# GpSimd's softplus split into three steps and the first norm's chain into two, in a two-layer recurrent and attention kernel with a new order of steps

## The reference, cut to what matters

```
xn = layernorm(x)
s  = mamba_block(xn)            # layer norm, in_proj, 4-tap causal conv, silu, x_proj,
                                # dt = softplus(dt @ dt_proj_w + dt_proj_b), selective scan over time,
                                # gate, out_proj, then layer norm + gelu FFN
g  = fp4_mlp(xn)                # three linear layers whose inputs are quantized to FP4 in blocks of 16
x  = x + s * silu(g)
xn = layernorm(x)
s  = attention(xn)              # over the batch axis (2 positions), 16 heads
g  = three residual blocks      # linear, layer norm, exact gelu, linear
x  = x + s * silu(g)
```

## Time and profile before

| | |
|---|---|
| median of 3 runs | 1763.05 us (1762.28 to 1764.01) |
| the profiled execution's own time | 1760.51 us |
| its span, first to last instruction | 1757.8 us |
| granted TensorE clock, mean | 0.951 |
| DVE busy | 1559.0 us (89%) |
| PE busy | 1537.0 us (87%) |
| ACT busy | 1437.1 us (82%) |
| POOL busy | 1251.3 us (71%) |

### The profile page before, as it was taken

The page is one execution under the profiler, slowest core; times in us unless marked ns, Lnnn a source line. Parts: engine busy times, 40 slices in busy tenths (PEclk is TensorE's granted clock), DMA queues, the critical chain, the costliest instruction groups (busy, mean ns, idle before and its releaser), DMA issues.

```text
span 1757.8 us, 26243 instructions
## 1 busy us (share of the span) xinstructions
PE 1537.0 (87%) x7512; PEld 1153.3 (66%) x7512; DVE 1559.0 (89%) x2887; ACT 1437.1 (82%) x3076; POOL 1251.3 (71%) x1314
## 2 busy tenths in 40 slices
PE   3766888989898998989898998989898998999875
PEld 2354767767676776667676776767676776777653
DVE  4889999999999999999999999999999999999711
ACT  2466888888998988898998988898998988898632
POOL 2557668787787769687787768687777869686422
PEclk8577999999999999999999999999999999999987
DMA  8111111111111111111111111111111111111100
GB/s 206 51 35 51 46 58 48 49 55 55 43 49 56 54 50 55 49 54 54 44 49 55 52 53 55 50 55 49 42 57 52 47 61 55 43 56 48 31 0 12
DMA packets 68452, 91.58 MB, mean 52 GB/s; under 512 B 15742, under 2 KB 34758, under 8 KB 68310
## 3 DMA queue, kind: packets, MB, share of 16 engines
q1 hardware_dynamic: 64566, 89.73, 17.0%
q10 hardware_dynamic: 3744, 0.18, 0.1%
HBM read 85.17 MB, written 4.72 MB: 51 GB/s over the span
## 4 chain that ended last, share of the span: by engine, by line
POOL 27%; PE 25%; DVE 17%; ACT 16%; issue 13%; DMA 1%; POOLq 0%; ACTq 0%; SPq 0%; DVEq 0%
POOL drive L796 10%; PE bank L339 10%; PE bank L455 6%; DVE unit L960 4%; POOL wide L845 3%; DVE hc L967 2%; ACT unit L571 2%; PE y_ps L365 2%; POOL wide L850 2%; POOL wide L847 2%; ACT hx L550 1%; ACT ops L537 1%; DVE xc L992 1%; ACT L537 1%; PE bank L326 1%
## 5 line engine op out<-in xcount | busy, mean ns | idle before, releaser
L796 POOL TENSOR_TENSOR drive<-wx,rows 128x1024 f32<-128x1024 f32 x256 | 603.6, 2358 | 154.8 <-DMA rows<-rows_scratch 78.5
L960 DVE TENSOR_TENSOR_SCAN unit<-unit,drive 128x512 f32<-128x512 f32 x512 | 616.4, 1221 | 36.5 <-POOL drive L803 27.7
L571 ACT ACTIVATE unit<-dt,aneg 128x254 f32<-128x254 f32 x1024 | 441.8, 468 | 8.0
L967 DVE TENSOR_TENSOR hc<-unit,rows 128x512 f32<-128x512 f32 x512 | 340.5, 683 | 5.6
L365 PE MATMUL y_ps<-ident,hc 128*128 128x128 f32 x2048 | 275.3, 280 | 65.8 <-DVE hc L967 65.7
L365 PEld LDWEIGHTS y_ps<-ident,hc 128*128 128x128 f32 x2048 | 239.1, 144 | 120.0 <-DVE hc L967 79.2
L339 PE MATMUL bank<-w_l,ops 128*128 128x256 f32 x768 | 194.0, 397 | 15.0 <-DVE xc L995 8.9
L339 PEld LDWEIGHTS bank<-w_l,ops 128*128 128x128 f32 x768 | 144.8, 195 | 65.5 <-DVE xc L995 20.5
L571 ACT ACT_TABLE_LOAD x109 | 139.8, 1283 | 1.9
L580 ACT ACTIVATE carry<-unit 128x4 f32<-128x4 f32 x512 | 79.1, 169 | 67.5 <-DVE unit L974 62.8
L455 PE MATMUL bank<-ops,w_f 128*128 128x256 f32 x512 | 116.2, 386 | 10.9 <-ACT ops L537 10.9
(11 more groups left out here) (229 smaller groups left out, 3150.0 us busy)
## 6 DMA issues: line engine op xcount, KB each, us to landing
rows<-rows_scratch SPq DMA_DIRECT2D x256, 256.0 KB, 3.4
x_t<-in_L_attn_x_dram SPq DMA_DIRECT2D x16, 256.0 KB, 3.8
xs<-in_L_attn_x_dram SPq DMA_DIRECT2D x16, 256.0 KB, 3.5
out_dram<-xs SPq DMA_DIRECT2D x16, 256.0 KB, 2.2
w_f<-in_L_attn_ffn_w_dram SPq DMA_DIRECT2D x2, 1024.0 KB
ops<-in_L_ffn_qweights_dram SPq DMA_DIRECT2D x1, 1536.0 KB, 15.2
w_in<-in_L_attn_in_proj_w_dram SPq DMA_DIRECT2D x1, 1024.0 KB, 5.2
hq_t<-attn_in_proj_weight_dram SPq DMA_DIRECT2D x1, 768.0 KB
```

Source lines behind the costliest of these rows:

```text
L571: last = a_.activation(u[:, k * TOK:(k + 1) * TOK].rearrange("p (b t) -> p b t", b=B)[:, :, 1:TC], dt[p][:, g, :].rearrange("p (b t) -> p ...
L796: g_.tensor_tensor(drive[n % 2][:, :, :].rearrange("p (g b) t -> p g b t", b=B), wx[p][:, :, :].rearrange("p g (b t) -> p g b t", b=B), ro ...
L960: v.tensor_tensor_scan(u[:, :], u[:, :], d, 0.0, ALU.mult, ALU.add).then_inc(S["scan_done"], 1)
L967: v.tensor_tensor(hc[n % NPROD][:, 4 * half:4 * half + 4, :].rearrange("p (g b) t -> p g b t", b=B), unit_of(ch, n, half)[:, :].rearrange( ...
```

## The change

Three things change. The three instructions of `log` become steps `log0`, `log1` and `log2`; the chain `f` becomes `fa` (five instructions) and `fb` (five), with the same waits. No instruction is added to POOL or removed. Then all five tables are new. They also begin at another place of the period, so that the signs of many words differ without a change of order.

```
-    "POOL": ("f", "log"),
+    "POOL": ("fa", "fb", "log0", "log1", "log2"),
...
-            elif name == "f":
+            elif name == "fa":
                 pool.wait_ge(*at("f_stats", ch))
                 pool.wait_ge(*at("xhf_done", ch - 1))
...
                 g_.tensor_tensor(r[0], r[3], epsc[:, :], ALU.add).then_inc(S["f_small"], 1)
+            elif name == "fb":
+                mean, var = f_mv[:, :, 0], f_mv[:, :, 1]
+                r = [f_sm[:, k, :] for k in range(8)]
                 pool.wait_ge(*at("f_small", ch, 5))
...
-            elif name == "log":
+            elif name == "log0":
                 pool.wait_ge(*at("sp_act", ch, 1))
                 g_.tensor_scalar(tmp_u, wx[p][:, :, :], 1.0, -1.0, ALU.add, ALU.add).then_inc(S["sp_pool"], 1)
+            elif name == "log1":
                 pool.wait_ge(*at("sp_pool", ch, 1))
                 g_.tensor_tensor(tmp_u, wx[p][:, :, :], tmp_u, ALU.subtract).then_inc(S["sp_pool"], 1)
+            elif name == "log2":
                 pool.wait_ge(*at("sp_pool", ch, 2))
                 pool.wait_ge(*at("dt_act", ch))
                 g_.tensor_tensor(tmp_u, tmp_u, dt[p][:, :, :], ALU.add).then_inc(S["sp_pool"], 1)
```

Two lines of the tables, of DVE:

```
-    clr10b hc11b clr11a attn- clr11b h1- scan12a hc12a scan12b hc12b clr12a clr12b scan13a hc13a clr13a f++
+    clr11b- attn-- scan12a- hc12a- h1-- scan12b- clr12a- hc12b- scan13a- clr12b- hc13a- f+ clr13a- scan13b-
```

More of the change, by code:

```diff
@@ L75 @@
 PE_PLAN = """
[L76 to L79, removed]
+    xn1T-- xi2 xi3 sum7- z1 b0a-- kv-- xp sum8- dt0 q-- b0T-- hqT0- dt1 sum9- b0b-- v1-- hqT1- sum10- sum11-
+    hqT2- h1T-- ctxT-- sum12- b1a-- b2b--- sum13- dn- sum14- b1T-- sum15- ao-- xqT ygT0- skip ygT1- g00 sum0 g01
@@ L80 @@
+    op- sum1 u00 u01 b1b-- g10 sum2 g11 u2T- u10 u11 sum3 h2T-- f10- f11- sum4 f12- f13- b2a-- uT+ sum5 f2-
+    b2T-- sum6 xi0+ xi1+ z0+
 """
 ACT_PLAN = """
[L82 to L85, removed]
@@ L86 @@
-    f13- exp6b out5b u+ exp7a b2n-- out6a exp7b out6b exp8a out7a exp8b b2g-- tap0+ tap1+ hn- z0+ xn1- tap2+
-    tap3+ z1+ out7b out8a xc0+ xc1+ exp9a exp9b out8b exp10a b0n- kv- xp+ out9a out9b exp10b exp11a dt0+ out10a
-    exp11b hq0 b0g- aexp- dt1+ out10b v1- dtexp+
+    b0g-- aexp-- hq0- dt1 v1-- dtexp out10b- exp12a- out11a- out11b- hq1- exp12b- exp13a- out12a- exp13b- hq2-
+    h1-- ctx-- out12b- exp14a- out13a- dtln exp14b- out13b- exp15a- first out14a- out14b- exp15b- b1n-- exp0a
+    gatec--- out15a- gatem- b1g-- exp0b out15b- s1-- xq exp1a out0a out0b yg0- exp1b exp2a yg1- out1a exp2b g00
@@ L89 @@
+    g01 out1b exp3a out2a exp3b out2b exp4a opn- g10 u2- out3a g11 exp4b out3b xn+ exp5a out4a exp5b h2-- out4b
+    exp6a f10- f11- out5a f12- xhf+ f13- exp6b u+ out5b exp7a out6a exp7b b2n-- out6b exp8a out7a exp8b b2g--
+    tap0+ tap1+ hn- z0+ out7b xn1- tap2+ tap3+ xc0+ out8a exp9a exp9b out8b xc1+ z1+ exp10a kv- xp+ b0n- usave+
+    out9a exp10b out9b exp11a out10a exp11b dt0+
 """
 POOL_PLAN = """
-    drive14- drive15- b1-- arg fix0 drive0 xout fin--- drive1 drive2 hb1-- drive3 fix1 f+ drive4 op- drive5 j0in
@@ L92 @@
-    hb2-- drive6 s0b- drive7 b2-- drive8 j0out j1in x1- drive9 drive10 diff- j1out b0- hb0- drive11 xin+ drive12
-    drive13 log+
+    arg drive15- fix0 b1-- drive0 xout fin--- drive1 drive2 fa+ hb1-- drive3 op- drive4 fb+ drive5 j0in hb2--
+    fix1 s0b- drive6 j0out drive7 j1in b2-- drive8 x1- drive9 drive10 diff- j1out hb0- b0- drive11 xin+ drive12
+    drive13 log0+ log1+ drive14 log2+
 """
 DVE_PLAN = """
-    clr15a- xround yg- scan0a clr15b- hc0a scan0b clr0a hc0b clr0b scan1a hc1a clr1a scan1b scan2a hc1b clr1b
@@ L102 @@
[L102 removed]
+    clr11b- attn-- scan12a- hc12a- h1-- scan12b- clr12a- hc12b- scan13a- clr12b- hc13a- f+ clr13a- scan13b-
+    scan14a- hc13b- dt clr13b- hc14a- scan14b- clr14a- hc14b- b1s-- wx clr14b- scan15a- scan15b- hc15a- hc15b-
+    clr15a- xround yg- scan0a clr15b- hc0a scan0b hc0b clr0a clr0b scan1a hc1a scan1b clr1a scan2a hc1b hc2a
+    scan2b clr1b op- hc2b ug0 clr2a scan3a clr2b scan3b h2-- hc3a scan4a hc3b clr3a hc4a clr3b scale0 ug1 scan4b
@@ L1258, in _ @@
                 unscale(1)
-                pool_step(pool, "log", 0)
+                for name in ("log0", "log1", "log2"):
+                    pool_step(pool, name, 0)
                 unscale(2)
```

23 lines of the change are left out of this document (13 added, 10 removed).

## The result

| | before | after |
|---|---|---|
| median | 1762.99 us (1762.28 to 1764.01, 4 runs) | 1776.44 us (1775.11 to 1779.43, 4 runs) |
| the profiled execution's own time | 1760.51 us | 1775.27 us |
| its span | 1757.8 us | 1773.5 us |
| mean granted clock | 0.951 | 0.955 |

The ratio after to before is 1.0078, interval 1.0061 to 1.0096: slower by 13 us or 0.8%, where 1776.0 us was forecast.

What follows compares the result with a forecast made beforehand. No engine is full: a loop through several binds, with DVE near its bound. Its links made a period 1.1 us longer; 1760.51 + 15.4 - 2.5 = 1773.4 us, 1776 us as median, range 1744 to 1797 us.

Steps and rivals of the forecast that it cites:

- link 2: From the end of `tap3` to the end of `exp12a` on ACT: two more table loads make DVE wait some 1.9 us.
- link 4: From the end of `clr14b` to the end of `exp0b` on ACT: 10.0 us, DVE waiting about 1 us for `scan0b`.
- the rule that the prediction set against link 2: Each switch of ACT's table set adds a drain of about 1380 ns; the two loads would cost 5.3 us.
- The 2.5 us added for the median: Step from the profiled execution's forecast, 1773.4 us, to the median of the runs, 1776 us.
- The ends: Filling unchanged; in the emptying `b1a` of chunk 15 goes ahead of `b2b` of chunk 14, 2.5 us gained (0 to 5).
- the front is the same work in the same order: At the kernel's beginning, the claim that nothing changes; the sum gives it no term.
- DVE stays the bound: Rival: the new order serves DVE, ACT being early at `exp12a` and `exp0b`; faster, 1742 us, chance 0.29.
- the scale: Times within one period, counted from the start of `conv0`; `exp12a` was forecast to end at 28.6.
- PE is drawn into the loop: Rival: clock dips and bank waits lengthen every period by a further 1.0 us; 1790 us, to 1798, chance 0.15.
- The split: On POOL, `drive14` ahead of `log2` ends the wait of `scan14a`: worth 0.5 us a period, the division itself costing nothing.
- Bubbles: On DVE, seven fewer dependent neighbours at some 0.12 us: 0.8 us a period gained if nothing else binds.
- link 3: On DVE, from `scan12a` to the end of `clr14b`, with `h1`, `dt` and `wx` now ahead of it: 16.1 us.

Runs made afterwards that it cites:

- e1: The kernel before, in its old order, with the divided steps and `drive14` between `log1` and `log2`: 1758.54 us, ratio 0.9981.
- e5: Changed kernel with `xc1`, `z1` ahead of `exp9a`, `b0s` ahead of `scan9a`, `b0` ahead of `hb0`, `v1` ahead of `b0b`: 1759.89 us, ratio 0.9985.
- e2: Changed kernel with `z1` and `xc1` back ahead of `exp9a` on ACT, two table loads fewer: 1787.48 us, ratio 1.0151.
- e6: Changed kernel with the softplus whole again on POOL, `log0`, `log1`, `log2`, then `drive14`: 1809.10 us, ratio 1.0266.
- e9: e5 with `h1` put back ahead of `scan12a` on DVE: 1757.58 us, ratio 0.9982.
- e10: e9 with `dt` two steps later on DVE, behind `clr13b` and `hc14a`: 1758.64 us, ratio 0.9990.
- e7: Changed kernel with `exp0b` and `out15a` ahead of `gatec`, `gatem` and `b1g` on ACT: 1794.74 us, ratio 1.0177.
- e8: e1 with `drive1` ahead of `fin` on POOL, and `s1`, `yg0` behind `xq` and the state 1 exponentials on ACT: 1806.84 us, ratio 1.0245.
- e12: e1 with DVE's `f` moved ahead of `scan1a`, `gatec` beside `gatem`, `out14b` and `exp0a` ahead of `first` on ACT: 1765.53 us, ratio 1.0026.

## Why the prediction was right, and where its reasons were not

**The sum.** The terms for one period against the trace of after, from `conv0` at 932.91 us; link 2 ends with `exp12a`, link 4 with `exp0b`:

| link | predicted us | measured us |
|---|---|---|
| 1, to the end of `tap3` | 5.5 | 5.5 |
| 2, to the end of `exp12a` | 23.1 | 23.2 |
| 3, `scan12a` to the end of `clr14b` | 16.1 | 16.2 |
| 4, to the end of `exp0b` | 10.0 | 10.2 |
| 5, to the start of `op` | 5.0 | 5.1 |
| 6, `op` to the end of `f2` | 36.3 | 36.0 |
| 7, to the next `conv0` | 3.6 | 3.6 |
| period | 99.6 | 99.7 |

(The measured links are rounded one by one.) One slip of addition stands in link 4: its terms as listed make 10.25 us, not 10.0, and 10.2 were measured. The signs named ahead were there: waits at `scan12a` and `scan0b` in nearly every period, none for POOL, 18 table loads a period, a last stretch of 93.8 us behind `yg` (94 to 95 said, 96.9 before). Behind each of the two new table loads the next instruction starts within 0.02 us, so they take 1.30 us each, as priced, and not the 5.3 us together of the rule that the prediction set against link 2.

**How near the number is, and what of that is luck.** Fourteen periods were to give +15.4 us and gave +15.9. But an undisturbed period grew by 1.25 us, not 1.1, which alone is 17.5; the filling and the disturbed periods, of which the sum said nothing, gave 1.6 back. Against the profiled execution 1773.4 us were said and 1775.3 measured. The 2.5 us added for the median were 1.2 in the kernel after. So the sum is borne out to about 2 us; that 1776 and 1776.4 agree within 0.5 us is luck.

**The ends.** The emptying took 3.1 us less behind the last `yg` (2.5 said), but that does not show the reason given, `b1a` ahead of `b2b`. e1, which has before's order there, takes 91.9 us for the 96.9 of before and the 93.8 of after. The mean granted clock in that stretch is 0.83 before, 0.86 after and 0.87 in e1, so the stretch before was long for another reason too. From the end of the last `f2` to the start of `b1a`, where the order acts, it is 27.1 us before, 24.8 after and 25.1 in e1: beside e1, the new order gains 0.3 us. The stretch from the last `conv0` to that `yg` took 5.4 us more, where nothing was expected, and e1 has 3.3 of them without a change of order. Together the two ends and what lies outside the span came to -1.1 us in place of -2.5. The beginning is 2.5 us shorter, and that is the order's: the first `conv0` comes at 138.7 to 140.7 us in all nine kernels with the new order, at 142.4 to 144.4 in the five with before's. Which step does it was not tried; the text's "the front is the same work in the same order" left out that the first pass of the new table already runs beside it.

**Link 2's size was right, its reason only in part.** The text put 2.6 us of it down to two table loads, 0.5 to `v1` and 0.1 to handovers. The forecast of 1.9 us of waiting is met as 0.69 at `attn` and 1.22 at `scan12a`. The small terms were not as said: ACT waits for `v1` only some 0.2 us (0.56 us lie between the starts of the last `dt1` copy and of `v1` above, 0.35 in e5), and its 0.23 us of waiting at `b0n` was put at nothing; the two errors cancel. "The same steps" holds nearly: `out7b` has left the link and `usave` (0.2 us) has come in. And taking the loads away (e2) gained nothing, since `z1` and `b0n` then waited in their place. Three things were late together: ACT's loads, POOL's `b0` behind `hb0` with DVE's later `b0s`, and `v1` on PE. Undone alone, the loads give 0 and the `b0` steps 0.35 us, both together 0.6, all three 0.76 of the 1.25 us (`v1` was not undone alone). What the text had wrong is the two table loads as the one cause. The arithmetic held because it took the old idle time (1.15 and 0.91 us) out of the link and counted ACT's work alone, and the idle time was what the new order had filled.

**The rival "DVE stays the bound"** was to win if `exp12a` ended before 27.2 us on the scale; it ended at 28.7. e5 brings it to 27.9 and the kernel to 1759.9 us. "PE is drawn into the loop" was partly there: five of 14 periods are 100.9 to 101.2 us, as four were 100.0 to 100.3 before, without becoming the rule. The text's reading of before's four waits for `q` was not quite right: three (1.75 and 1.76 us) fall on a dip of the clock, the fourth (0.36) does not, and the dips at 566, 962 and 1263 us lie in periods of 98.5 us.

**The split.** "Worth 0.5 us a period" is 0.54 in the old order (e1). In the new order the text had no separate price for it; e6 shows 1.7 us in an undisturbed period and 33 us in all, disturbed periods included.

**Bubbles.** Of the 0.8 us for seven fewer dependent neighbours the sum used 0.4, in link 3, which came out as forecast; no run isolated it, so it is not shown. DVE's busy time fell by 13 us (1559.0 to 1546.0), which bought nothing, as DVE waits.

**What stays open.** With the three causes and `h1` back (e9) the period is 98.8 us, against 97.9 for e1, which has before's order whole. The remaining 0.9 us lie behind `scan12a`: `attn` ends 26.8 us behind `conv0` in both, `b1n` starts at 45.5 in e9 and at 44.5 in e1. `dt`'s place by itself is not the cause (e10). `b1` behind `fix0` on POOL, for which `b1n` waits, and `exp0a` and `gatec` between `b1n` and `exp0b` on ACT, are left, and were not undone alone.

## What to carry to other kernels

When an order changes on all engines at once, put the sum along one closed loop, at the new table's steps but the old trace's durations, and count work apart from idle time; seven links here came out within 0.4 us each, though in link 2 two small terms were wrong and cancelled. Don't name one cause for a late step until it has been undone alone: steps in a tuned pipeline are late in ties, and each restoration shows only what the next tied one leaves. And before a step that reads a rotating bank is moved later on its engine, look three results ahead on the producer: three of the experiments (e7, e8, e12) cleared the wait in view and stopped PE for 2 to 3.4 us instead.

## What the runs showed of the hardware

**A dip of the clock costs by where it falls.** In every kernel here TensorE's granted clock is at times 0.5, its lower level of 1.2 GHz, in stretches of 3.4 or 6.8 us. Most of the disturbed periods have one where PE computes `q`. In e6, windows at the full clock and at the lower, with PE busy throughout, and PE's product for `q` in the latter (3.57 us, where eight such matmuls take 1.9 to 2.0 otherwise):

```profile
961.00:964.40 3.40, 3.35 (x12) 1.28 (x10) 3.37 (x7) 3.36 (x6) 2.79 (x4) 1.00 0.00 0
968.10:971.50 3.40, 3.40 (x9) 2.19 (x8) 2.11 (x2) 3.18 (x9) 3.38 (x3) 0.50 0.08 28
```

```profile
967.88 3.57 PE L340 MATMUL bank<-w_qkv,ops 128*128 128x256 f32 x8
```

DVE waits for that product in `score`:

```profile
971.98 0.69 DVE L1064 TENSOR_TENSOR prod<-bank,kv 128x512 f32<-128x512 f32 x1 [1.76 <-PE bank L345]
```

Such a period is 1.3 us longer in e6, 1.2 in after and 1.6 to 1.8 before. Elsewhere a dip is free. In after, the five dips that begin 17 to 18 us behind `conv0` lie in the periods of 100.9 to 101.2 us. Four more begin 32 to 33 us behind it, and their periods are 99.72 to 99.74 us, undisturbed ones, though PE's transposes for `sumN` take 1.94 us in one of them and 1.09 in a period without a dip:

```profile
966.17 1.09 PE L366 MATMUL y_ps<-ident,hc 128*128 128x128 f32 x8 [0.33 <-DVE hc L973]
...
1065.92 1.94 PE L366 MATMUL y_ps<-ident,hc 128*128 128x128 f32 x8
```

In e10 each of the eleven periods from 332 to 1420 us has one, 22 or 32 us behind `conv0`, and they last 98.85 to 98.88 us. How many dips there are differs from order to order: between 180 and 1680 us of the profiled execution the clock was at the lower level for 51 us before, 48 after, 71 in e1, 24 in e5, 75 in e6 and 80 in e10. The dips on `q` are a likely reason that e1, with a period 1.0 us shorter than e5's, is only 1.4 us faster in the median. Ahead of the dip in e6 PE had stood for 1.27 us, waiting for ACT (965.55 to 966.82 us), and then had been busy for 1.3 us at the full clock; why one order has few and another many was not settled.

**A tiny operation of POOL is stretched beside DVE's wide one.** The first step of a root on POOL (two columns) takes 0.20 us elsewhere; beside DVE's `wx` (1024 columns, both inputs in SBUF, 976.61 to 977.80 us in after) it took 1.02:

```profile
976.83 1.02 POOL L778 TENSOR_TENSOR b_sm<-b_mv,epsc 128x2 f32<-128x2 f32 x1 [0.24 <-DVE b_mv L924]
```

So it is in all 14 periods, and beside DVE's scans and `hc`, which read one input from PSUM, the same instruction takes 0.20 us every time. It is the same in before, where such an instruction took 1.08 us beside `dt`. Four dependent ones in a row make a root, so its place against `dt` and `wx` is worth 0.8 us to ACT's norm behind it.

**And a tiny operation of DVE beside POOL's wide one.** One period of before is 100.0 us long without a dip and without a wait for `q`. In it a `drive` came late, since it had waited 7.43 us for its rows:

```profile
1212.32 2.36 POOL L796 TENSOR_TENSOR drive<-wx,rows 128x1024 f32<-128x1024 f32 x1 [7.43 <-DMA rows<-rows_scratch]
```

DVE's first instruction of `scale1` behind the maximum (44 columns) started beside it, at 1213.02 us, and took 1.71 us, to 1214.73, where it takes 0.18 to 0.22 in the others behind the filling; POOL's ended at 1214.68. These 1.5 us are the whole excess of that period.
